# A selective-scan block in fp32 on one core: row statistics in pieces, the normalised rows and their transposes elsewhere in a chunk's first and last steps, and another TensorE order of output parts, sums and dt

## The reference

```python
# block 1
h = layernorm(x);  xi, z = split(h @ in_proj_w)          # 1024 -> 2 x 2048 channels
xc = silu(causal_conv4(xi) + conv_b)
dt_r, B, C = rmsnorm of the three parts of (xc @ x_proj_w.T)   # 64, 16 and 16 columns
dt = softplus(dt_r @ dt_proj_w.T + dt_bias);  A = -exp(A_log)
# for each channel d and state n, over time t
hs[t] = exp(dt*A) * hs[t-1] + dt*B*xc;   ys[t] = sum_n hs[t] * C
x = x + ((ys + D*xc) * silu(z)) @ out_proj_w.T
# block 2
x = x + layernorm(x) @ dequantised(W).T + bias
```

## Time and profile before

| | us |
|---|---|
| median of 3 runs | 4699.61 (4698.31 to 4702.74) |
| the profiled execution | 4697.21 |
| its span (first to last instruction) | 4695.4 |
| PE busy, share of span | 4448.9, 95% |
| DVE | 4160.0, 89% |
| POOL | 4039.2, 86% |
| ACT | 3542.4, 75% |

### The profile page before, as it was taken

The page is one execution under the profiler, slowest core; times in us unless marked ns, Lnnn a source line. Parts: engine busy times, 40 slices in busy tenths (PEclk is TensorE's granted clock), DMA queues, the critical chain, the costliest instruction groups (busy, mean ns, idle before and its releaser), DMA issues.

```text
span 4695.4 us, 80181 instructions
## 1 busy us (share of the span) xinstructions
PE 4448.9 (95%) x26656; PEld 4049.0 (86%) x26656; DVE 4160.0 (89%) x5745; ACT 3542.4 (75%) x8848; POOL 4039.2 (86%) x2942
## 2 busy tenths in 40 slices
PE   7788989999999999999999999999999999999889
PEld 6567879989898998989989898998989889898779
DVE  3898989989899998989989899998989989899981
ACT  3777787877778787777877878787787777778760
POOL 0898989989898998989989898998989899899990
PEclk9889999999999999999999999999999999999999
DMA  7324243353434435343353534334353443434232
GB/s 255 130 79 161 99 159 139 114 186 133 173 129 161 145 138 175 124 178 128 123 188 123 177 137 165 137 128 173 138 180 120 145 165 129 165 127 155 90 115 94
DMA packets 160285, 678.56 MB, mean 145 GB/s; under 512 B 21120, under 2 KB 30080, under 8 KB 110720
## 3 DMA queue, kind: packets, MB, share of 16 engines
q1 hardware_dynamic: 141440, 639.88, 39.0%
q10 hardware_dynamic: 18432, 33.56, 1.9%
HBM read 618.32 MB, written 55.05 MB: 143 GB/s over the span
## 4 chain that ended last, share of the span: by engine, by line
PE 59%; DVE 20%; POOL 7%; issue 6%; ACT 5%; DMA 1%; SPq 0%; DVEq 0%; POOLq 0%; ACTq 0%
PE g L767 13%; PE gx L594 13%; PE ys L574 12%; DVE hb L1342 11%; PE ys L614 9%; PE g L689 4%; POOL dbx L486 4%; DVE hc L1290 4%; DVE gx L1238 2%; POOL half L494 2%; PE ys L604 2%; DVE bst L1218 2%; PE gx L581 2%; ACT hb L1061 1%; PE hb L853 1%
## 5 line engine op out<-in xcount | busy, mean ns | idle before, releaser
L1342 DVE TENSOR_TENSOR_SCAN hb<-hb,dbx 128x512 f32<-128x512 f32 x2048 | 2498.0, 1220 | 108.0 <-ACT hb L1061 84.4
L486 POOL TENSOR_TENSOR dbx<-dtx,bb 128x1024 f32<-128x1024 f32 x1024 | 2421.0, 2364 | 60.1 <-DVE hb L1342 34.9
L1061 ACT ACTIVATE hb<-dt,a_neg 128x256 f32<-128x256 f32 x4096 | 1789.5, 468 | 66.3
L494 POOL TENSOR_TENSOR half<-hc 128x512 f32<-128x512 f32 x1024 | 1303.1, 1273 | 135.4 <-DVE hc L1290 120.4
L1290 DVE TENSOR_TENSOR hc<-hb,cb 128x512 f32<-128x512 f32 x2048 | 1378.9, 673 | 0.0
L574 PE MATMUL ys<-half,ident 128*128 128x256 f32 x4096 | 1073.2, 389 | 133.4 <-POOL half L494 119.2
L574 PEld LDWEIGHTS ys<-half,ident 128*128 128x128 f32 x4096 | 757.2, 194 | 254.3 <-POOL half L494 151.3
L767 PEld LDWEIGHTS g<-wo,ybuf 128*128 128x128 f32 x7680 | 954.0, 198 | 20.2 <-issue 1.3
L767 PE MATMUL g<-wo,ybuf 128*128 128x128 f32 x7680 | 966.7, 281 | 0.6 <-issue 0.6
L614 PE MATMUL ys<-xnT,wz 128*128 128x256 f32 x4096 | 928.8, 380 | 1.6 <-DVE ybuf L1301 1.6
L594 PE MATMUL gx<-xnT,wx 128*128 128x256 f32 x3968 | 904.5, 381 | 4.3 <-DMA wx<-in_win 2.6
(11 more groups left out here) (105 smaller groups left out, 2766.1 us busy)
## 6 DMA issues: line engine op xcount, KB each, us to landing
wz<-in_win SPq DMA_DIRECT2D x128, 1024.0 KB, 4.8
wx<-in_win SPq DMA_DIRECT2D x124, 1024.0 KB, 4.8
wo<-in_wout SPq DMA_DIRECT2D x123, 1024.0 KB, 4.9
wf<-wf_scratch SPq DMA_DIRECT2D x113, 512.0 KB, 3.2
xc_scratch<-xcn ACTq DMA_DIRECT2D x128, 256.0 KB, 2.1
xcs<-xc_scratch SPq DMA_DIRECT2D x128, 256.0 KB, 5.0
bb<-bc_scratch SPq DMA_DIRECT2D x64, 512.0 KB, 7.5
cb<-bc_scratch SPq DMA_DIRECT2D x64, 512.0 KB, 6.7
```

Of the source, the lines that this page charges most:

```text
L486: nc.gpsimd.tensor_tensor(dbx[:, k % 2, :].rearrange("p (n t) -> p n t", n=NQ), dtx[:, S % 2, a, :].unsqueeze(1).to_broadcast([P, NQ, T]), ...
L494: nc.gpsimd.tensor_tensor(half[:, k % 4, :], hc[:, k % 2, 0:HALF], hc[:, k % 2, HALF:GW], ALU.add).then_inc(halves, 1)
L1061: ins = nc.scalar.activation(h[:, m * T:(m + 1) * T], dt[:, j % 2, a, :], ACT.Exp, scale=a_neg[:, ds((2 * j + a) * N + 2 * v + m, 1)])
L1342: nc.vector.tensor_tensor_scan(h[:], h[:], dbx[:, k % 2, w * UW:(w + 1) * UW], 0.0, ALU.mult, ALU.add).then_inc(scans, 1)
```

## The change

- *Statistics in pieces.* The four pieces of the first norm stand one each in steps 1 to 4 and its aggregation in step 5, all behind `add_out`; of the second norm one piece each in steps 5 and 6, two and the aggregation in step 7. Each piece signals `l1_dve` or `l2_dve`; the aggregation waits for its four. A semaphore increment (`aggr_go`) is gone.
- *Rows on ScalarE.* The first norm's start and rows move from behind units 14 and 15 of step 6 to behind units 8 to 10. In a first step the second norm's start moves behind unit 2 and its rows behind units 6 and 7; the copies of the norm2 transposes move behind units 8 to 11, those of norm1 (step 7) one unit later.
- *TensorE order.* In all steps `out_proj(1)` goes ahead of `x_proj`, and `out_proj(2)` goes behind `group(3)` and `dt_proj`. First steps with an `ffn` put the norm2 transposes among output parts 2 and 3, groups 1 to 3 and `dt_proj`, and `x_in_proj` last. Last steps with a norm1 spread its transposes over output parts 0 and 1 and group 0.
- *In these two kinds of step* (`edge`) the taps stand behind product 13 on VectorE and behind unit 14 on ScalarE. In last steps with a norm1, `y_gate(S, 0)` goes behind product 11.

TensorE, after the common head `ffn, late_group(6), late_group(7)` and ahead of the common end `z_in_proj(1), group(4), z_in_proj(0), group(5)`:

```diff
-                    if first and st.ffn or last and st.norm1:
-                        norm2(0)
+                    if last and st.norm1:
                         norm1(0)
                         x_proj()
+                        out_proj(0)
+                        norm1(1)
+                        group(0)
+                        norm1(2)
+                        out_proj(1)
+                        norm1(3)
+                        x_in_proj(0)
+                        group(1)
+                        ss_transpose()
+                        x_in_proj(1)
+                        group(2)
+                        group(3)
+                        dt_proj()
+                        out_proj(2)
+                        out_proj(3)
+                    elif first and st.ffn:
+                        out_proj(0)
+                        out_proj(1)
+                        x_proj()
+                        group(0)
+                        out_proj(2)
+                        norm2(0)
+                        out_proj(3)
+                        group(1)
                         norm2(1)
-                        norm1(1)
-                        out_proj(0)
+                        group(2)
+                        dt_proj()
                         norm2(2)
-                        norm1(2)
-                        group(0)
+                        group(3)
                         norm2(3)
-                        norm1(3)
+                        x_in_proj(0)
+                        x_in_proj(1)
                     else:
                         out_proj(0)
+                        out_proj(1)
                         x_proj()
-                    out_proj(1)
-                    if not (first and st.ffn or last and st.norm1):
                         group(0)
-                    x_in_proj(0)
-                    group(1)
-                    ss_transpose()
-                    x_in_proj(1)
-                    group(2)
-                    out_proj(2)
-                    group(3)
-                    dt_proj()
-                    out_proj(3)
+                        x_in_proj(0)
+                        group(1)
+                        ss_transpose()
+                        x_in_proj(1)
+                        group(2)
+                        group(3)
+                        dt_proj()
+                        out_proj(2)
+                        out_proj(3)
```

ScalarE and VectorE, the core:

```diff
+                    edge = first and st.ffn or last and st.norm1
                     unit(0)
                     unit(1)
+                    unit(2)
                     norm2_start()
-                    norm2_row(0)
-                    unit(2)
-                    norm2_row(1)
                     unit(3)
...
                     silus()
-                    norm2(0)
-                    norm1(0)
                     unit(4)
                     first_skip_term()
-                    norm2(1)
+                    norm1(0)
+                    unit(5)
                     norm1(1)
-                    unit(5)
-                    norm2(2)
+                    unit(6)
+                    norm2_row(0)
                     norm1(2)
-                    unit(6)
-                    norm2(3)
+                    unit(7)
+                    norm2_row(1)
                     norm1(3)
-                    unit(7)
                     rms_square()
                     unit(8)
+                    norm2(0)
                     rms_apply()
+                    norm1_start()
                     unit(9)
+                    norm2(1)
+                    norm1_row(0)
                     unit(10)
+                    norm2(2)
+                    norm1_row(1)
                     unit(11)
+                    norm2(3)
                     ss_out()
                     unit(12)
-                    x_taps()
+                    if not edge:
+                        x_taps()
                     dt_softplus()
...
                     unit(14)
-                    norm1_start()
-                    norm1_row(0)
+                    if edge:
+                        x_taps()
                     unit(15)
-                    norm1_row(1)
```

```diff
+                    def norm_stats():
+
+                        if st.norm1 and 1 <= j <= 4:
+                            norm1_piece(c + 2, j - 1)
+                        if st.norm1 and j == 5:
+                            norm1_aggregate(c + 2)
+                        if st.outproj and j in (5, 6):
+                            norm2_piece(c - 1, j - 5, 0)
+                        if st.outproj and last:
+                            norm2_piece(c - 1, 0, 1)
+                            norm2_piece(c - 1, 1, 1)
+                            norm2_aggregate(c - 1)
...
                     product(8)
-                    if pre and st.norm1:
-                        norm1_stats(c + 2)
                     scan(10)
                     product(9)
-                    y_gate(S, 0)
+                    if not (last and st.norm1):
+                        y_gate(S, 0)
                     scan(11)
                     product(10)
                     scan(12)
                     product(11)
-                    taps()
+                    if last and st.norm1:
+                        y_gate(S, 0)
+                    if not edge:
+                        taps()
                     scan(13)
                     product(12)
                     add_out()
-                    norm2_stats()
+                    norm_stats()
                     scan(14)
                     product(13)
+                    if edge:
+                        taps()
                     scan(15)
                     product(14)
```

More of the change, by code:

```diff
@@ L215, in build_program @@
         xp_add, o_add, f_add = sem("xp_add"), sem("o_add"), sem("f_add")
-        rms_red, l1_dve, l1_stats, l2_dve, l2_stats, aggr_go = (sem("rms_red"), sem("l1_dve"), sem("l1_stats"),
-                                                                sem("l2_dve"), sem("l2_stats"), sem("aggr_go"))
+        rms_red, l1_dve, l1_stats, l2_dve, l2_stats = (sem("rms_red"), sem("l1_dve"), sem("l1_stats"),
+                                                                sem("l2_dve"), sem("l2_stats"))
         deq_a, deq_b, a_ready = sem("deq_a"), sem("deq_b"), sem("a_ready")
@@ L1214, in _, with aggregate @@
         def _(dve):
-            def stats(rows, bst, mv, mid, done, n):
-                for tt in range(TT):
-                    for h in range(2):
-                        ins = nc.vector.bn_stats(bst[:, tt, 6 * h:6 * h + 6], rows(tt, h))
-                ins.then_inc(mid, 1)
-                dve.wait_ge(mid, after(n))
-                dve.sem_inc(aggr_go, 1)
+            def aggregate(bst, mv, mid, done, n):
+                dve.wait_ge(mid, after(4 * n))
                 for tt in range(TT):
@@ L1224, in stats, with norm1_piece, norm1_aggregate @@
                 ins.then_inc(done, 1)
+            def norm1_piece(chunk, i):
+                tt, h = divmod(i, 2)
+                dve.wait_ge(xrow_in, landed(chunk + 1))
+                dve.wait_ge(l1_stats, after(chunk))
+                nc.vector.bn_stats(bst1[:, tt, 6 * h:6 * h + 6], xrow[:, tt, h * 512:(h + 1) * 512]).then_inc(l1_dve, 1)
+            def norm1_aggregate(chunk):
+                aggregate(bst1, mv1, l1_dve, l1_stats, chunk + 1)
             def norm1_stats(chunk):
-                dve.wait_ge(xrow_in, landed(chunk + 1))
-                stats(lambda tt, h: xrow[:, tt, h * 512:(h + 1) * 512], bst1, mv1, l1_dve, l1_stats, chunk + 1)
+                for i in range(4):
+                    norm1_piece(chunk, i)
+                norm1_aggregate(chunk)
             def pair_conv(q):
@@ L1273, in block_add, with norm2_piece, norm2_aggregate @@
                                         ).then_inc(done, 1)
-            def norm2_stats_of(chunk):
-                dve.wait_ge(o_add, after(PAIRS * (chunk + 1)))
-                rows = x2[:, chunk % 2, :]
-                stats(lambda tt, h: rows[:, tt * H + h * 512:tt * H + (h + 1) * 512], bst2, mv2, l2_dve,
-                      l2_stats, chunk + 1)
+            def norm2_piece(chunk, tt, h):
+                dve.wait_ge(o_add, after(PAIRS * chunk + 4 * (h + 1)))
+                dve.wait_ge(l2_stats, after(chunk))
+                nc.vector.bn_stats(bst2[:, tt, 6 * h:6 * h + 6],
+                                   x2_rows(chunk % 2)[:, tt, h * 512:(h + 1) * 512]).then_inc(l2_dve, 1)
+            def norm2_aggregate(chunk):
+                aggregate(bst2, mv2, l2_dve, l2_stats, chunk + 1)
             def times_c(SU, u):
@@ L1386, in rms_sums @@
                             chunk_sums(c + 1)
-                    def norm2_stats():
-                        if last and st.outproj:
-                            norm2_stats_of(c - 1)
+                    def norm_stats():
[9 more added lines that the diff above has]
+                            norm2_aggregate(c - 1)
```

(6 more changed lines are left out.)

## The result

The changed kernel takes 4654.43 us (median of 4 runs, 4652.27 to 4656.87) against 4699.67 before: ratio 0.9903, 95% interval 0.9887 to 0.9918. It is faster by 45 us where the forecast was 77.6: inside the range for 8 in 10 (4590 to 4665), outside the forecast's own (4608 to 4638). The profiled execution has a span of 4650.4 us.

| stretch | before | after | forecast of the difference | measured |
|---|---|---|---|---|
| prologue and chunk 0 | 393.8 | 392.3 | -1 | -1.4 |
| chunk 1 | 283.5 | 272.4 | -6.6 and a boundary | -11.0 |
| chunks 2 to 13 | 3357.4 | 3302.7 | 12 x -5.2 = -62 | -54.6 |
| chunk 14 | 273.2 | 271.1 | a boundary and -2 with chunk 15 | -2.1 |
| chunk 15 | 261.1 | 276.9 | with chunk 14 | **+15.9** |

A forecast was written before the change was run, and what follows sets the result against it. TensorE's throughput was taken to bound ordinary steps, with waits and half clock at boundaries. Won: 68 (13 boundaries) + 6.6 (chunk 1) + 3 (boundaries of chunks 0 and 14) = 77.6, so 4622 us; own range 4608 to 4638, 8 in 10 4590 to 4665.

The forecast's parts named there:

- a boundary: Step 7 of a chunk and step 0 of the next: waits 5.05 us instead of 10.3, 5.2 won, x 13 = 68.
- What bounds: An ordinary step is bound by TensorE's throughput alone, 33.20 us; work alone would take 269.6 us a chunk.
- Pieces: Statistics in pieces over steps 1 to 7: cost 0, as an ordinary step has 1.6 us of slack on VectorE.
- Step 7: A chunk's last step: TensorE waits 1.5 us together, scan 13 waits 1.7, next scan 0 at +37.4.
- Step 0: A chunk's first step: TensorE waits 1.35 for `y`, 1.15 for rows, 1.05 for a copy, together 3.55 us.
- The clock: Step 0: idles under 1.4 us and 6 us or more apart, so no half clock.
- rival 1: The clock still falls in step 0 and gives back 36 us: 4658 us; chance 0.15.
- rival 4: GpSimd's half sum 3 late in ordinary steps, or `wo` late in step 1: 26 us, 4648; chance 0.08.
- Chunk 1: Chunk without `ffn`, where TensorE and VectorE wait for each other: 6.6 us won in steps 1 to 6.
- Price 0: Ordinary steps: `out_proj(2)` behind `group(3)` and `dt_proj` costs nothing; 0.4 us a step if sum 3 came late.

## Why the prediction was right, and where it was wrong

*What bounds.* Right, when steps are cut by TensorE's `ffn`. Ordinary steps are then at 33.20 in the kernel before, the changed one and with either order (33.31 with the pieces and the old order), and the 269.6 us of pure work stands: 275.2 after with 5.7 of waits at a boundary, 272.65 with 3.1.

*Pieces.* Right that they cost nothing in ordinary steps of chunks 2 to 13 beside the new order; with the old one they cost 0.1 us a step there and 5.5 us in chunk 1. They win 1.6 us a chunk alone and 1.4 on top of the rest. The burst was said to make the wait of 2.42 for half 7; without it 1.12 of it are left.

*Step 7.* 1.5 us of waits forecast, 1.65 measured, among them 0.88 for the copy ahead of `x_in_proj(0)` (0.75 forecast). Scan 13 waits 2.47 for 1.7, and next scan 0 comes at 38.06 for 37.4.

*Step 0.* 3.55 forecast, 4.1 measured by start-to-start distances in the timeline of chunk 9, with other shares: 0.8 for `y` instead of 1.35, 0.5 for the rows instead of 1.15, 0.95 for the copy instead of 1.05, and two that I had excluded, 0.7 for half 7 and 1.15 for half 3. The last was missed because `group(3)` of a first step was only compared with TensorE's own pace. Together 5.7 instead of 5.05; the chunks won 4.55 us for 5.2. What the prediction never asked is what the old first step would lose behind the new step 7: 1.5 us instead of 4.1. It counted the new first step into the gain without that comparison, and this part of the change costs 2.5 us a boundary.

*The clock* stayed up in step 0 of chunks 3 to 14, as forecast; in chunk 2's it fell (PEclk of the step 0.91, behind an idle of 2.69). That 4654 lies by rival 1's 4658 is chance: its mechanism did not happen. The range held the result because it reached past rival 1, and the loss that filled it is one that no rival names. Of rival 4, GpSimd's half 3 is late in a first step and not in an ordinary one of chunks 2 to 13, and in step 1 of chunk 9 TensorE has no wait for `wo`.

*Chunk 1.* Right in direction, too small: its steps 1 to 6 take 9.0 us less for 6.6 (8.3 less by the order alone), its two ends the other 2.1. VectorE's wait for sum 3 falls as forecast, 12.8 us in steps 1 to 5 to 3.6, but the steps are not at 33.2: they alternate between 32.3 with PEclk 1.00 and 34.0 with 0.95, where all had 0.95. So part of the gain is the clock, which the sum for chunk 1 left out.

*The step that failed* is "Price 0" for the order in ordinary steps. It was argued from steps in which TensorE never waits, and applied to all. In steps 1 to 7 of chunk 15 TensorE has 7.8 us less to do (6.9 of the input projection, 0.9 of `x_proj`) and already waited for halves 1 and 2; there `out_proj(2)` had filled a wait, and moved behind sum 3 it lengthens the chain and leaves three idles in a row, behind which the clock halves. Measured price: 15.9 us in chunk 15 and 8.3 in the tail, 24 of the 32 us by which the forecast was off; the old order put back there alone wins 23.5. The trace of the kernel before showed these waits in chunk 15 (1.33 and 2.70) and a clock already at 0.95, and the prediction read no row of it. The other 8 us are the boundaries of chunks 2 to 13.

The rule of the page "TensorE: Matmul & The Clock Gate" of the Trainium skill, section "A second HAM failure mode: psum-queue depth-cycling" (short idles between groups of matmuls can make the clock swing), which I weighed and set aside, agrees with the rows of chunk 15 (0.85 with idles like 1.33, 2.70 and 2.01) and did not show in step 0 of chunks 3 to 14 (1.00 with idles up to 1.11).

The granted clock is not told by the idles alone. With the statistics in bursts, idles of 0.24 or 0.25 and 1.57 or 1.58 us at the same two places left it at 1.00 in the first step of chunks 6 and 12 and lowered it (0.95) in those of chunks 7 and 10.

*Open.* With the first step as before a boundary wins 7.1 us; pieces alone and the ordinary order alone give 1.6 and 0. The other 5.5 us were not split further between TensorE's order in step 7, the late early `y_gate` and the place of the first norm's rows. The rows point at the two parts working together: scan 0 of step 7 is 1.76 us behind its `ffn` before, 1.11 with the pieces alone, 1.39 with the ordinary order alone (1.26 ahead in the steps before, until the burst of step 6), and 0.67 ahead with both. No run has these two and nothing else, so this is not shown. Chunks 2 to 13 of the changed kernel, which run the same program, take between 274.5 and 276.0 us each, so effects of a few us in the sum of twelve are not told apart here.

## What to carry to other kernels

A price of zero "because the busiest engine hides it" holds only for the iterations in which that engine is busiest: look at the first and the last ones, where part of its work is missing, before the order inside the loop is changed for all. Cut a loop's time by the starts of the engine that sets the pace: cut by another engine's, a loss can show in the step next to its own. Where an engine waits several times in a row, spread its free work between the waits, and keep nothing behind the last that could stand ahead of it. When a change makes two repairs of one stall, try each without the other: here the change without the second was 34 us faster.

## What was not expected of the hardware

Eight useless matmuls in each of two places of a step made it 2.2 and 3.0 us shorter in steps 3 and 4 of chunk 15, with TensorE's granted clock at 1.00 instead of 0.85. The same idles, some 0.25 and 1.57 us, lowered the clock in some first steps and not in others. A transfer of 0.5 MB that landed 5.0 us after its issue with 1.5 MB of earlier loads still to land took 11.0 us with 3 MB.
